# One vision-transformer block on one core: an order changed in five places of the schedule

## The reference

```python
h = layernorm(patches @ W) * gamma                                # 320 -> 256
x = layernorm(h)
q, k, v = silu(x @ Wq), silu(x @ Wk), x @ Wv                      # 16 heads of 64
cum = cumsum(-softplus(x @ Wa + ba), over the tokens of an image)
decay[i, j] = exp(cum[i] - cum[j]) where j <= i, else 0
o = ((q k^T) * decay) v
o = (o - mean) / sqrt(var + eps) * gn_w + gn_b                    # per head, over tokens and width
h = h + (o * sigmoid(x @ Wg)) @ Wo
h = h + the two experts of eight (256 -> 1024 -> 256, gelu) that the router picks, weighted
```

## Time and profile before

| | us |
|---|---|
| median of 3 runs | 1246.43 |
| lowest and highest run | 1241.35, 1247.16 |
| the profiled execution | 1245.03 |
| its span | 1243.0 |
| PE busy in it | 1212.2 |
| DVE, ACT, POOL busy | 824.3, 859.9, 427.2 |
| bytes moved | 194.46 MB |

### The profile page before, as it was taken

How to read it: one execution, slowest core, us unless ns; L and a number is a source line. 1 busy time by engine, 2 the same in 40 slices (tenths; PEclk the granted TensorE clock), 3 DMA queues, 4 the chain that set the end, 5 groups by cost and what they waited for, 6 DMA issues and landing times.

```text
span 1243.0 us, 27365 instructions
## 1 busy us (share of the span) xinstructions
PE 1212.2 (98%) x8554; PEld 1068.5 (86%) x8554; DVE 824.3 (66%) x2127; ACT 859.9 (69%) x2019; POOL 427.2 (34%) x521
## 2 busy tenths in 40 slices
PE   8999999999999999999999999999999999999997
PEld 6788788788788788888878878989999999899996
DVE  5555666666766666667667577567888888465653
ACT  4767667667668668667668567547888888666663
POOL 2212212242242242242152142463445444443433
PEclk8999999999999999999999999999999999999999
DMA  5532332342333233243233237498987876988984
GB/s 194 174 107 78 89 105 83 92 137 81 96 118 101 90 112 112 75 126 113 71 121 110 75 106 231 143 283 227 284 237 221 253 216 192 257 273 242 282 253 98
DMA packets 125607, 194.46 MB, mean 156 GB/s; under 512 B 16272, under 2 KB 91504, under 8 KB 125360
## 3 DMA queue, kind: packets, MB, share of 16 engines
q1 hardware_dynamic: 110864, 175.37, 44.1%
q0 software_dynamic: 13584, 17.26, 7.0%
q10 hardware_dynamic: 1056, 0.55, 0.2%
HBM read 167.40 MB, written 29.05 MB: 158 GB/s over the span
## 4 chain that ended last, share of the span: by engine, by line
PE 86%; DMA 4%; ACT 4%; issue 3%; DVE 2%; POOL 1%; ACTq 0%; another core or an unknown queue 0%; SPq 0%; POOLq 0%; DVEq 0%
PE bank L1235 21%; PE bank L1593 11%; PE bank L1581 11%; PE bank L1228 7%; PE bank L1321 7%; PE bank L1277 4%; PE bank L1293 4%; PE bank L1185 3%; DMA out<-mid_f,tok 3%; PE bank L1606 2%; PE bank L1395 2%; PE bank L1620 2%; ACT dec_x L872 2%; PE bank L1297 2%; PE bank L1408 2%
## 5 line engine op out<-in xcount | busy, mean ns | idle before, releaser
L1235 PE MATMUL bank<-xn_sp,big_r 128*128 128x512 f32 x1152 | 299.1, 402 | 0.9 <-DVE dec_x L1770 0.9
L1235 PEld LDWEIGHTS bank<-xn_sp,big_r 128*128 128x128 f32 x1152 | 209.8, 189 | 48.2 <-issue 1.3
L689 POOL TENSOR_SCALAR_AFFINE_SELECT dec_x<-dec_x 128x256 f32<-128x256 f32 x256 | 106.4, 443 | 372.1 <-DMA dec_x<-cum_scratch 372.0
L872 ACT ACTIVATE dec_x<-dec_x,ncum 128x256 f32<-128x256 f32 (+1 forms) x512 | 186.5, 445 | 10.4 <-POOL dec_x L689 10.4
L1581 PE MATMUL bank<-big_r 128*128 128x256 f32 x1296 | 167.6, 286 | 0.0
L1581 PEld LDWEIGHTS bank<-big_r 128*128 128x128 f32 x1296 | 160.5, 192 | 0.9
L1770 DVE TENSOR_TENSOR dec_x<-bank,dec_x 128x384 f32<-128x384 f32 x256 | 124.9, 549 | 37.6 <-PE bank L1280 31.5
L746 POOL DMA_INDIRECT out<-mid_f,tok x68 | 113.6, 1671 | 63.6 <-DMA out<-mid_f,tok 28.6
L740 POOL TENSOR_SCALAR mid_f<-mid_f,dec_x 128x256 f32<-128x256 f32 x68 | 72.5, 1070 | 160.2 <-DVE mid_f L2031 157.7
L943 ACT ACTIVATE mid_f<-bank,h 128x256 f32<-128x256 f32 x216 | 101.1, 478 | 33.7 <-PE bank L1581 19.4
L2063 DVE TENSOR_TENSOR big_r<-mid_f,big_r 128x256 fp32r<-128x256 f32 x216 | 90.6, 423 | 32.6 <-ACT big_r L963 32.0
(11 more groups left out here) (244 smaller groups left out, 2187.9 us busy)
## 6 DMA issues: line engine op xcount, KB each, us to landing
big_f<-in_L_ffn_w SPq DMA_DIRECT2D x68, 1024.0 KB, 8.0
dec_x<-cum_scratch SPq DMA_DIRECT2D x128, 384.0 KB
big_w<-in_L_ffn_w SPq DMA_DIRECT2D x12, 1024.0 KB, 8.4
mid_f<-expert_rows SPq DMA_DIRECT2D x27, 261.0 KB
h_scratch<-h SPq DMA_DIRECT2D x16, 256.0 KB
h<-h_scratch SPq DMA_DIRECT2D x8, 512.0 KB, 4.0
out<-h SPq DMA_DIRECT2D x16, 256.0 KB, 4.4
xt<-in_x SPq DMA_DIRECT2D x14, 256.0 KB, 3.3
```

What stands on the lines that cost most here:

```text
L689: pool.affine_select(out=d, in_=d, pattern=[[0, 2], [1, P]], compare_op=ALU.is_ge, fill=fill, base=0, channel_multiplier=-1).then_inc(M["c ...
L872: act.activation(d, d, ACT.Exp, bias=ncum[p % 2][:, NS * u + s, 2 * c + hh:2 * c + hh + 1]).then_inc(M["exp_done"], 1)
L1235: mm = pe.matmul(bank[target][:, :], wp[:, k, c * P:(c + 1) * P], xp[:, k, :], start=(k == 0 and j == 0), stop=(k == EC - 1 and j == 2))
```

## The change

Five places, all of them a matter of order or of how many filler matmuls run; no product, reduction or transfer is added or left out besides these fillers (five at one place become two at three places).

1. The start: SP loads the third image only after the embedding weights and image 0 are there; POOL waits for image 0 before seven of its constants; DVE embeds both images before it norms either; ACT rounds the second weight ahead of its first copy; PE has its fillers in three places and `tokens(2)` ahead of the turns.
2. ACT's step 1: the copy of the turned image ahead of the eight exponentials.
3. DVE's `place` in two halves, the first before `silu_k` of step 2, the second and the slots after it.
4. `gated(p-1, 1, 1)` from the end of DVE's step 2 into step 3 before `silu_q`, and ACT's `y_hi(p-1, 1, 1)` from before `tanh_q` to before `tanh_k` of step 3. At the last step of pair 6, ACT takes `tanh_g(7, 0)` ahead of `y_hi(6, 0, 0)`.
5. `mixed_row`: `row_tails` behind hidden chunk 3 in place of chunk 2.

```diff
@@ SP, start
             load_patches(1)
-            load_patches(2)
             sp.wait_ge(M["wt_in"], 32)
             sp.wait_ge(M["xt_in0"], 32)
+            load_patches(2)
             load_weight(0)
@@ POOL, start
             pool.dma_start(ones[:, :], ones_d).then_inc(M["c_sum"], 16)
+            pool.wait_ge(M["xt_in0"], 32)
             for dst, src in ((strict, strict_d), (half, half_d), (gnw, gn_w), (gnb, gn_b),
@@ ACT, last_step
-                y_hi(p, 0, 0)
+                if pair(p + 2) or not nxt:
+                    y_hi(p, 0, 0)
                 if nxt:
                     tanh_g(p + 1, 0)
+                    if not pair(p + 2):
+                        y_hi(p, 0, 0)
                     y_hi(p, 0, 1)
@@ ACT, step
-                if c == 3 and post:
-                    y_hi(p - 1, 1, 1)
                 if c == 6:
                     affined(p, 0, 0)
                 tanh_q(p, c + 1)
...
                     keep_v(p, {1: 4, 2: 6, 3: 7}[c], 2)
+                if c == 3 and post:
+                    y_hi(p - 1, 1, 1)
                 tanh_k(p, c + 1)
...
+                if c == 1 and nxt:
+                    keep_xnT(2 * p + 2)
                 if late:
                     decay(p, c + 1, 0)
                 decay(p, c + 1, 1)
...
                 if c == 1 and nxt:
-                    keep_xnT(2 * p + 2)
                     scaled_h(2 * p + 2)
@@ ACT, start
             weight_hi(0)
+            weight_hi(1)
             keep_xnT(0)
-            weight_hi(1)
             keep_xnT(1)
@@ PE, start
             pe.wait_ge(M["c_sum"], 32)
-            keep_running(5)
+            keep_running(2)
+            tokens(2)
+            keep_running(2)
             turn(0)
-            tokens(2)
             turn(1)
+            keep_running(2)
             logits(0)
@@ DVE, place
-            def place(p):
+            def place(p, half):
-                for t in range(TP):
+                for t in range(NS * half, NS * half + NS):
...
+                if half == 0:
+                    return
                 dve.wait_ge(M["rsel_done"], TP * TOPK * (p + 1))
@@ DVE, step
+                if c == 3 and post:
+                    gated(p - 1, 1, 1)
...
                 if c == 2 and routed:
-                    place(p - 2)
+                    place(p - 2, 0)
...
-                if c == 2:
-                    if post:
-                        gated(p - 1, 1, 1)
+                if c == 2 and routed:
+                    place(p - 2, 1)
@@ DVE, start
             embed(0)
+            embed(1)
             embed_norm(0)
-            embed(1)
             embed_norm(1)
@@ DVE, mixed_row
                     if c == 2:
                         keep_y(before, pieces)
+                    if c == 3:
                         row_tails(k, rows_f[0], BS)
```

More of the change, by code:

```diff
@@ L2206, in _ @@
             weigh(p - 1)
-            place(p - 1)
+            place(p - 1, 0)
+            place(p - 1, 1)
             residual(2 * p)
@@ L2219, in _ @@
             keep_ranks(p)
-            place(p)
+            place(p, 0)
+            place(p, 1)
             keep_y(whole(1), BS)
```

## The result

| us | before | after |
|---|---|---|
| median, first comparison (5 executions each) | 1246.43 | 1231.48 |
| lowest and highest | 1240.66, 1250.68 | 1230.41, 1232.86 |
| the profiled execution, its span | 1245.03, 1243.0 | 1230.41, 1228.4 |
| median, second comparison (11 and 6) | 1243.71 | 1231.60 |
| lowest and highest | 1241.06, 1248.64 | 1229.52, 1233.11 |

The ratio is 0.9893, 95% interval 0.9869 to 0.9917, in the first comparison and 0.9896 (0.9875 to 0.9916) in the second. The change gives 12 to 15 us. The time forecast, 1231, is the time measured; the sum behind it holds only in part.

What follows compares the result with a forecast made beforehand. PE was taken as the bound, busy 1212.2 of 1243.0 us. Terms 1.9 + 2.5 + 4.3 + 4.4 + 0.5 + 2.6 - 1.0 = 15.2 us took the profiled 1245.0 to 1229.8, the median to 1231; range 1226 to 1239.

Steps and rivals of the forecast that it cites:

- The copy, 4.3 us: ACT's step 1: PE's seven 0.6 us waits for the copy go whole, 4.3 us, ends 3.0 and 4.3.
- Places and gate product 4.4: Scores of step 3: PE's gaps close in pairs 2 to 6 and partly in pair 7, 4.4 us, ends 2.0 and 4.6.
- pair 6 0.5: Last step of pair 6: the value product's wait for tanh of the gates goes, 0.5 us, ends 0 and 0.5.
- The gap of pair 7: PE's gap of 1.04 us before the scores of step 3 in pair 7; 0.83 of it taken as won.
- The 0.3 us by which ACT's rounding doesn't fit: Step 3: y rounding of 1.05 us before tanh of k, where ACT idles 0.76; the excess was said to just fit.
- give-back of 1.0: Steps 3 and 4: 1.0 us subtracted for late masks, q and k, and ACT's rounding, ends 0 and 3.
- Start, the order, 1.9 us: Kernel start: embedding both images first brings image 1's norm and what follows forward, 1.9 us, ends 1.0 and 2.9.
- all that follows hangs on this norm: Start: turn, ACT's copy, logits and running sums were all said to follow image 1's norm, 1.8 us sooner.
- Start, the clock, 2.5 us: Start: fewer PE idle gaps keep the clock up through the value products, 2.5 us, ends 0 and 2.5.
- Rival one: Start: the clock falls all the same, the gain loses 2.5 us, median 1233.7; chance 0.16.
- The rule cited in the forecast: Start: the number of low-clock matmuls varies from run to run, so the median would gain about half, 1.2 us more time.
- Row tails, 2.6 us: Mixed blocks, second layer: of PE's 3.6 us of waits behind adds in memory 2.6 are won, ends 0.9 and 3.6.

Runs made afterwards that it cites:

- a_both: Changed kernel with image 2 loaded ahead of SP's first waits and ACT's two copies ahead of its second rounding; ratio 0.9896 (0.9871 to 0.9920).
- a_soft: a_both with the softplus of the decays ahead of ACT's third rounding; median 1231.67 us, ratio 0.9896 (0.9875 to 0.9916).
- parts_only: Kernel before with copy, places in halves, gate product, y rounding and pair 6 swap, start and tails as before; 1233.64 us beside 1243.78, ratio 0.9920.

## Why the prediction was right, and where its steps were not

- **The copy, 4.3 us:** right. All 4.3 us of waits are gone; by the marks it is 4.5 us alone and 4.9 on top of the other part (765.30 less 760.39).
- **Places and gate product 4.4, pair 6 0.5:** right in mechanism and nearly in size: waits of 4.6 and 0.5 are gone, and by the marks both are 4.5 alone and 4.9 on top of the copy. The gap of pair 7 closed whole, where 0.83 of its 1.04 had been taken: the forecast had counted four reductions at 0.166 us each, but in the trace of before they start 0.21 us apart (345.19, 345.40, 345.61 in pair 3), so that four of them and the slots are 1.0 us. The 0.3 us by which ACT's rounding doesn't fit delayed nothing: no wait before the scores of step 4 came up. The **give-back of 1.0** was too much: the two parts together made 9.3 to 9.7 us, with 4.3 + 4.4 + 0.5 = 9.2 forecast before any give-back.
- **Start, the order, 1.9 us:** wrong in size. The forecast named what stands against it, two image pieces ahead of the first weight and the second rounding ahead of the copy, and left its sum at 1.9. They take most of it: the logits begin at 20.4 on average in the five profiles with the new order of ACT, SP and DVE (20.0 to 20.6), after 21.0 in the six with the old one (20.6 to 21.8), and first scores stand at 36.6 on average (the four without added fillers) after 36.8. DVE's part came true and more: its begin stands at 8.7 to 9.4 after 10.0 to 11.2 in these profiles, its second norm at 15.7 after 18.8 on average, 3.2 us sooner. The failed step is that all that follows hangs on this norm; in the new order the logits hang on ACT's list. With that out of the way, in a_both and a_soft, they begin 2.2 us behind the norm, as they did before the change (18.36 and 20.55).
- **Start, the clock, 2.5 us:** wrong. The granted clock fell in both profiles of the changed kernel, and in all five with its start, one of them with more fillers. Rival one, with chance 0.16, is what happened to this term. How long it stays low differs between executions of an equal start: 10, 7, 3, 3, 7 and 7 us with the old one. Profiles with the clock low for 7 us have their first scores at 36.6 on average with the new order (four) and at 37.0 with the old (three), so at equal clock the order is worth some 0.4 us; with the old order the two with 3 us stand at 35.8. The rule cited in the forecast (the Trainium skill, TensorE: Matmul & The Clock Gate, What's actually happening) says for the first slow matmuls of a kernel that their number varies from run to run. These traces show such a variation in another place: the granted clock was 1.00 for the first 20 us in all 14 profiles, and what varies is the fall behind that. So the profile of before, with 10 us at 1.2 GHz, showed the worst case of six, and the forecast priced it as the normal one.
- **Row tails, 2.6 us:** not shown. In some profiles the wait is gone; by the mixed stretch the seven profiles with tails behind chunk 3 average 165.2 and the six with the old place 166.7, 1.5 us less, but each group spreads over 4 to 5 us. By time it is 0.2 and -0.4 us in two comparisons. Against the forecast, the wait doesn't have one size: it depends on when the adds in memory land.

The sum of what was measured is 9.4 for the pairs, 0.2 and 1.5 by the averages of the marks: 11.1, beside 12.1 by the medians. The forecast had 15.2. It hit the time by luck, because its starting point was about as much too high: the profiled execution (1245.0) and the median of three runs (1246.43) lay above what longer series gave, 1242.67, 1243.71, 1243.78 and 1244.53. Taken from 1243.7, its own sum would have said 1228.5, which is 3 us too fast and still in the range. The chance of faster by over 0.5% was rightly high, since the 9.2 us of gaps that return in every pair are 0.7% alone.

None of the variants beat the changed kernel. Open stays where the tails' gain went in the executions that have no profile, whether start and tails together give the 2 us between parts_only and the changed kernel, and whether chunk 4 would be a better place for the tails; that wasn't tried.

## What to carry to other kernels

Price a gap by how often it returns: the two that stood in six or seven of the eight pairs gave 9.4 of 12.1 us and added up, while the ones seen once in one trace (start, mixed blocks) were a draw from a spread as wide as themselves. When an engine's work is pulled forward, look at what the next engine has listed ahead of its use of it; and before something is moved back in a list, find the transfer that is issued right behind it and the first use of what that brings.

## What was not expected of the hardware

The same adds in memory took 7.25 and 8.23 us from issue to release, and in schedules that are equal there the mixed stretch took from 163.2 to 167.5 us; in the pair compared above the adds account for all of it. The granted clock was at 1.2 GHz for 0 to 10 us of the start in 14 profiles; it stayed at 2.4 GHz through a stretch in which PE was busy for 1.07 of 2 us (a_soft), and fell in another in which it was busy for 1.74 of 2 us (the changed kernel, from 20 us on, 0.57).
